# Causal attention: the mask is added by VectorE on the way to SBUF instead of by a matrix product on TensorE

## The reference, cut to what matters

```
q = (x @ w_q).reshape(bs, n, h, hd); k = ...; v = ...      # 16 heads of 64
dot = jnp.einsum('bqhd,bkhd->bhqk', q * scale, k * scale)
causal = jnp.tril(jnp.ones((n, n), dtype=bool))
dot = jnp.where(causal, dot, -inf)
att = jax.nn.softmax(dot, axis=-1)
out = jnp.einsum('bhqk,bkhd->bqhd', att, v).reshape(bs, n, h * hd)
return out @ w_u + b_u
```

## Time and profile before

| | |
|---|---|
| median of 3 runs | 1931.3 us (1929.0 to 1939.09) |
| the profiled execution | 1936.66 us, span 1934.9 us |
| granted TensorE clock, mean | 0.969 |
| causal stage in the span | from the first transfer at 4.57 us to the last addition at 367.2 us |
| PE busy | 1807.5 us of the span (93%) |
| DVE, ACT, POOL busy | 1334.9, 658.5, 266.6 us |

### The profile page before, as it was taken

The page is one execution under the profiler, slowest core; times in us unless marked ns, Lnnn a source line. Parts: engine busy times, 40 slices in busy tenths (PEclk is TensorE's granted clock), DMA queues, the critical chain, the costliest instruction groups (busy, mean ns, idle before and its releaser), DMA issues. The chain is left out here.

```text
span 1934.9 us, 44403 instructions
## 1 busy us (share of the span) xinstructions
PE 1807.5 (93%) x17091; PEld 1540.5 (80%) x17091; DVE 1334.9 (69%) x3641; ACT 658.5 (34%) x1523; POOL 266.6 (14%) x200
## 2 busy tenths in 40 slices
PE   5999999789877999999999889988999999999998
PEld 4888788567666888988888777767888888888887
DVE  4656664467658888988988848855766666666664
ACT  2444443244353112202321236645333323233332
POOL 3222333301010000000000058811000000000000
PEclk9999999799878999999999989998999999999999
DMA  4000000222033000000000130001121111112101
GB/s 164 2 1 0 0 0 1 49 58 56 20 81 62 7 0 5 5 5 0 5 5 0 37 87 2 1 26 24 26 32 16 30 19 22 27 16 33 16 1 44
DMA packets 139265, 47.73 MB, mean 25 GB/s; under 512 B 108178, under 2 KB 138418, under 8 KB 139186
## 3 DMA queue, kind: packets, MB, share of 16 engines
q1 hardware_dynamic: 139186, 46.66, 10.6%
HBM read 42.43 MB, written 4.19 MB: 24 GB/s over the span
## 5 line engine op out<-in xcount | busy, mean ns | idle before, releaser
L2988 ACT ACTIVATE m_silu<-m_gate 128x512 f32<-128x512 f32 x136 | 81.4, 599 | 379.7 <-PE m_gate L630 379.7
L3069 DVE TENSOR_TENSOR m_act_up<-m_silu,m_up 128x512 f32<-128x512 f32 x136 | 93.5, 688 | 168.7 <-PE m_up L630 125.3
L3053 DVE SCALAR_TENSOR_TENSOR g_x<-m_y,m_combine,g_x 128x256 f32<-128x256 f32 x272 | 118.9, 479 | 52.1 <-PE m_y L630 50.5
L246 ACT ACTIVATE a_prob<-a_score,a_neg_max 128x128 f32<-128x128 f32 x256 | 90.4, 365 | 162.6 <-DVE a_neg_max L236 162.6
L630 PE MATMUL f_act<-f_hT_pair_high,f_kiT_high 128*128 128x256 f32 x448 | 127.5, 285 | 0.3
L2564 PE MATMUL f_out<-f_ko,f_gel 128*128 128x256 f32 x512 | 123.7, 390 | 2.1 <-issue 1.4
L630 PE MATMUL f_act<-f_hT_pair_low,f_kiT_high 128*128 128x256 f32 x448 | 124.4, 278 | 0.0
L630 PE MATMUL f_act<-f_hT_pair_high,f_kiT_low 128*128 128x256 f32 x448 | 123.8, 276 | 0.0
L2625 ACT ACTIVATE f_gel<-f_act 128x512 f32<-128x512 f32 x128 | 76.6, 598 | 122.9 <-PE f_act L630 102.4
L2564 PE MATMUL f_turn<-f_ko,f_gel 128*128 128x256 f32 x512 | 112.1, 379 | 0.0
L2564 PEld LDWEIGHTS f_turn<-f_ko,f_gel 128*128 128x128 f32 x512 | 97.2, 190 | 13.2
(11 more groups left out here) (439 smaller groups left out, 5201.6 us busy)
## 6 DMA issues: line engine op xcount, KB each, us to landing
f_gel<-in_L_ffn_key_in SPq DMA_DIRECT2D x16, 256.0 KB, 4.5
f_ko<-in_L_ffn_key_out SPq DMA_DIRECT2D x2, 2048.0 KB, 19.3
g_shared<-in_ctx SPq DMA_DIRECT2D x8, 256.0 KB, 2.7
fp_wq_nat<-in_L_ffn_w_q SPq DMA_DIRECT2D x8, 256.0 KB, 3.1
h_kept<-fp_hT SPq DMA_DIRECT2D x8, 256.0 KB, 2.6
g_shared<-h_kept SPq DMA_DIRECT2D x8, 256.0 KB, 3.0
g_ctx_next<-in_ctx SPq DMA_DIRECT2D x8, 256.0 KB, 2.6
g_ctx_all<-in_ctx SPq DMA_DIRECT2D x1, 2048.0 KB, 9.9
```

The costliest lines, as they stand in the source:

```text
L246: last = act.activation(self.prob[:, u % 4, j, :], self.score_bank[u % 2][:, j // 2, (j % 2) * P:(j % 2 + 1) * P], ACT.Exp, bias=self.neg_ ...
L2988: act.activation(silu[:, m, :], gate_bank[m][:, :], ACT.Silu).then_inc(silu_ready[m].sem, 1)
L3053: last = dve.scalar_tensor_tensor(x[:, tile, :], y_bank[n][:, t * D:(t + 1) * D], weight, x[:, tile, :], ALU.mult, ALU.add)
L3069: dve.tensor_tensor(act_up[:, m, :], silu[:, m, :], up_bank[m][:, :], ALU.mult) \
```

## The change

The two mask products per unit go. The score products write their banks directly. VectorE adds the mask, now one float32 block of 128x128 used for all four blocks of the unit, to the scores in PSUM and writes the sum into the unit's probability buffer in SBUF; it waits for its own addition, then takes the maximum from there. ScalarE reads its exponential's input from that buffer and writes the result over it. TensorE's wait before the scores of a unit is now for the addition of two units before (the banks have been read then), not for the exponentials. The wait for a free probability buffer moves from ScalarE's queue to VectorE's. `stage_constants` fills and cuts one matrix less, and the mask is 128x128. No transfer is added, removed or moved.

```diff
 pe_scores:
-            pe.wait_ge(self.exp_ready.sem, self.exp_ready.at(i, u - 1))
-        ident_bf, mask_bf = self.mask
-        for a in range(2):
-            pe.matmul(self.score_bank[n][:, a, 0:2 * P], ident_bf[:, :], mask_bf[:, :], start=True, stop=False,
-                      skip_group_check=True)
+            pe.wait_ge(self.masked.sem, self.masked.at(i, u - 1))
...
-                                 kT[par][rows, 2 * g + t, b * P:(b + 1) * P], start=False, stop=True,
+                                 kT[par][rows, 2 * g + t, b * P:(b + 1) * P], start=True, stop=True,
...
-    def dve_max(self, dve, i, u):
+    def dve_max(self, dve, i, u, first=False):
+
         dve.wait_ge(self.scored.sem, self.scored.at(i, u + 1))
-        dve.tensor_reduce(self.neg_max[:, u, :].rearrange("p (a t) -> p a t", a=2), self.head_scores(u % 2),
-                          AX.X, ALU.max, negate=True).then_inc(self.max_ready.sem, 1)
...
+        if not first:
+            dve.wait_ge(self.transposed.sem, self.transposed.at(i, u - 3 if u != 2 else 0))
+        prob = self.prob[:, u % 4, :, :]
+        dve.tensor_tensor(prob.rearrange("p (a t) k -> p a t k", a=2), self.head_scores(u % 2),
+                          self.mask[:, :].unsqueeze(1).unsqueeze(1).broadcast_to([P, 2, 2, P]), ALU.add) \
+            .then_inc(self.masked.sem, 1)
+        dve.wait_ge(self.masked.sem, self.masked.at(i, u + 1))
+        dve.tensor_reduce(self.neg_max[:, u, :], prob, AX.X, ALU.max, negate=True).then_inc(self.max_ready.sem, 1)
...
 act_exp:
-        if not first:
-            act.wait_ge(self.transposed.sem, self.transposed.at(i, u - 3 if u != 2 else 0))
         for j in range(4):
-            last = act.activation(self.prob[:, u % 4, j, :], self.score_bank[u % 2][:, j // 2, (j % 2) * P:(j % 2 + 1) * P],
-                                  ACT.Exp, bias=self.neg_max[:, u, j:j + 1], accum_out=self.row_sum[:, u, j:j + 1])
+            last = act.activation(self.prob[:, u % 4, j, :], self.prob[:, u % 4, j, :], ACT.Exp, bias=self.neg_max[:, u, j:j + 1], accum_out=self.row_sum[:, u, j:j + 1])
...
 stage_constants:
-            for m in (ident, ident_bf, causal_bf):
+            for m in (ident, causal_mask):
                 pool.memset(m[:, :], 0.0).then_inc(filled, 1)
...
-            for m in (ident, ident_bf):
-                pool.affine_select(out=m[:, :], in_=m[:, :], compare_op=ALU.not_equal, fill=1.0, base=0,
-                                   pattern=[[-1, P]], channel_multiplier=1)
...
-            pool.affine_select(out=causal_bf[:, :], in_=causal_bf[:, :], compare_op=ALU.is_ge, fill=NEG, base=0,
-                               pattern=[[0, 2], [-1, P]], channel_multiplier=1)
...
+            pool.affine_select(out=causal_mask[:, :], in_=causal_mask[:, :], compare_op=ALU.is_ge, fill=NEG, base=0,
+                               pattern=[[-1, P]], channel_multiplier=1)
```

More of the change, by code:

```diff
@@ L197, in __init__ @@
         self.scored = s.counting("scored", UNITS)
+        self.masked = s.counting("masked", UNITS)
         self.max_ready = s.counting("max_ready", UNITS)
@@ L343, in act_first @@
     def act_first(self, act):
-        self.act_exp(act, 0, 0, first=True)
-        self.act_exp(act, 0, 1, first=True)
+        self.act_exp(act, 0, 0)
+        self.act_exp(act, 0, 1)
     def on_act(self, act, i, before, after):
@@ L358, in dve_first @@
     def dve_first(self, dve):
-        self.dve_max(dve, 0, 0)
-        self.dve_max(dve, 0, 1)
+        self.dve_max(dve, 0, 0, first=True)
+        self.dve_max(dve, 0, 1, first=True)
         self.dve_normalise(dve, 0, 0)
@@ L383, in on_dve, with stage_causal_attention @@
             self.links.end()
-def stage_causal_attention(nc, x, ident, ident_bf, mask_bf, x_in, w_q, w_k, w_v, w_u, b_u, load_next):
+def stage_causal_attention(nc, x, ident, mask, x_in, w_q, w_k, w_v, w_u, b_u, load_next):
     HD = 64
@@ L412, in chunk_of @@
             return part[:, c // 2, 4 * (c % 2):4 * (c % 2) + 4, :].rearrange("p t q -> p (t q)")
-        att = CausalAttention(s, ident, (ident_bf, mask_bf), lambda c: chunk_of(attnT, c),
+        att = CausalAttention(s, ident, mask, lambda c: chunk_of(attnT, c),
                               vector_copies=(0, 2, 4, 6))
@@ L3085, in _, with stage_constants @@
             all_experts(dve, expert_on_dve)
-def stage_constants(nc, ident, ident_bf, causal_bf, head_mask, ones_row):
+def stage_constants(nc, ident, causal_mask, head_mask, ones_row):
     with ExitStack() as ctx:
@@ L3101, in _ @@
                 pool.memset(m[:, :], 1.0).then_inc(filled, 1)
-            pool.wait_ge(filled, 5)
-            for m in (ident, ident_bf):
-                pool.affine_select(out=m[:, :], in_=m[:, :], compare_op=ALU.not_equal, fill=1.0, base=0,
-                                   pattern=[[-1, P]], channel_multiplier=1)
-            pool.affine_select(out=causal_bf[:, :], in_=causal_bf[:, :], compare_op=ALU.is_ge, fill=NEG, base=0,
-                               pattern=[[0, 2], [-1, P]], channel_multiplier=1)
+            pool.wait_ge(filled, 4)
+            pool.affine_select(out=ident[:, :], in_=ident[:, :], compare_op=ALU.not_equal, fill=1.0, base=0,
+                               pattern=[[-1, P]], channel_multiplier=1)
+            pool.affine_select(out=causal_mask[:, :], in_=causal_mask[:, :], compare_op=ALU.is_ge, fill=NEG, base=0,
+                               pattern=[[-1, P]], channel_multiplier=1)
             pool.affine_select(out=head_mask[:, :], in_=head_mask[:, :], compare_op=ALU.is_ge, fill=0.0, base=0,
@@ L3124, in decoder @@
         stored = s.sem("stored")
-        ident_bf = s.sb("ident_bf", [P, P], BF16)
-        causal_bf = s.sb("causal_bf", [P, 2 * P], BF16)
+        causal_mask = s.sb("causal_mask", [P, P])
         shared = Shared(s, "shared", 3072)
```

6 lines of the change are left out of this document (3 added, 3 removed).

## The result

Median of 11 runs each: 1944.84 us after (1941.52 to 1951.07), 1934.44 before (1929.00 to 1939.09), ratio 1.0053 with a 95% interval of 1.0040 to 1.0066: 10.4 us longer. That is inside the wide range forecast (1926 to 1947), outside the range of the forecast case itself (1930 to 1943), and on the edge of the 0.5% (the interval lies on both sides of it). The profiled execution took 1943.92 us, span 1942.2, which is 7.3 more than before's 1934.9; the forecast was 4.0 more. In the experiments, the ratios leave out one run of e6 (9558.9 us) and one of before (2912.6 us) that stand far off.

A forecast was written before the change was run, and what follows sets the result against it. TensorE bounds steps 0 to 3, while DVE's chain ends level with it in steps 4 to 7. Sum: -6.2 + 7.0 + 3.1 + 0.7 - 0.6 = +4.0 us on 1931.3, 1935.3; range 1930 to 1943, wide 1926 to 1947.

The forecast's parts named there:

- forecast case: The prediction's own case for the whole kernel: 1935.3 us, range 1930 to 1943, chance 0.75.
- the pairs: Seven pairs before the last: 6.2 us won in steps 0 to 3, 7.0 lost in steps 4 to 7.
- the last pair: Final pair without ring work: six DVE additions lengthen the chain, 3.1 us later (2.3 to 4.4, slow clock perhaps 1 more).
- the start: Before the first pair: 0.7 us lost to DVE's additions and maxima, 0.6 won by GpSimd's smaller fills and selects.
- GpSimd blocks addition and maximum: Rival: GpSimd's splits also hold DVE's addition and maximum, delaying ScalarE's copy; +10 to +11 us, 1942; chance 0.08.
- the two handovers: Ring to scores in steps 0 to 3, 0.23 us won each; DVE's copy to transposes in steps 5 and 7, 0.50 late.
- T+0.09 to T+3.84: Steps 4 and 5, T being the ring's end: scores start at T+0.09, the next transposes at T+3.84, 0.50 us late.
- the 0.6 us that GpSimd wins at the start: Kernel start: one fill and one select fewer, and smaller ones, 0.6 us before the first transfer is issued.
- perhaps 1: Last pair: what a slow clock there might add, in us, on top of the 4.4 upper case.
- PE is the bound after all: Rival: all 64 units save 0.23 to 0.32 us and the addition hides everywhere; -15 to -20 us, chance 0.10.
- The clock falls in pairs 0 to 6: Rival: longer transpose waits in steps 5 and 7 bring half clock to some pairs; 1943 to 1960 us, chance 0.07.
- DVE's queue backs up: Layer normalisation behind longer step 5 delays a ring copy: 0.3 us more per pair, +6 in all, inside the range.

The follow-up runs named there:

- e6: The changed kernel with one more wait, so GpSimd's second output-weight split follows DVE's last input-weight subtraction; 1941.1 us, ratio 1.0036 to before.
- e5: The kernel before with one more wait, so GpSimd's second output-weight split follows DVE's last input-weight subtraction; 1928.7 us, ratio 0.9976.
- e12: The changed kernel with 20 unread filler products on PE between the scores of units 1 and 2 of the first pair; 1942.5 us, ratio 1.0035 to before.
- e1: The kernel before with its mask products removed and nothing in their place (softmax over unmasked scores); 1929.0 us, ratio 0.9974.
- e2: The changed kernel with the mask products of before put back, so the mask is added twice; 1952.8 us, ratio 1.0089 to before.
- e11: The kernel before, all masks by products, with DVE's and ScalarE's late steps reordered and GpSimd's second split made to wait; 1928.5 us, ratio 0.9973.
- e3: The changed kernel with DVE adding masks only for units 2 to 5, mask products elsewhere and in the last pair; 1935.9 us, ratio 1.0014 to before.
- e4: The changed kernel with mask products for units 0 and 1 of the first pair and 2 to 7 of the last; 1938.9 us, ratio 1.0029 to before.
- e7: The changed kernel, DVE normalising and copying before addition and maximum (steps 4, 6), ScalarE copying before exponentials (5, 7); 1940.8 us, ratio 1.0036 to before.
- e9: As e7, with DVE's copy of finished head outputs also ahead of addition and maximum in steps 4 and 6; 1935.4 us, ratio 1.0004 to before.

## Why the prediction came out as it did

**The size.** Forecast were 4.0 us more, measured 7.3 in the profiled executions and 10.4 in the medians. Of the terms of the sum, the pairs (0.8 forecast, 1.09 measured) came close, the last pair (3.1, measured 3.85) was sized too low, and the start (+0.1, measured 2.18) was wrong. The base of 1931.3, from three runs, lay 3.1 under the median of eleven. The other 3.1 us, between 7.3 and 10.4, are in no term. That 10.4 equals the +10 to +11 of the rival in which GpSimd blocks addition and maximum is coincidence: its mechanism didn't occur (below).

**Right:** the direction, the place, and the two handovers. A score group begins 0.21 behind the last ring product (about 0.1 of it gap, as taken from the earlier trace rows), which saves 0.24 against 0.23 predicted. In step 4 the transposes come 3.73 behind the scores' start (194.05 to 197.78), where the prediction had T+0.09 to T+3.84, 3.75. The transposes wait 1.20 and 1.29, the normalisation takes 1.60, the period is 41.95. The values product of step 7 starts at 209.87 without a wait, 0.77 behind the start of ScalarE's copy:

```profile
207.54 0.40 ACT L246 ACTIVATE a_prob<-a_prob,a_neg_max 128x128 f32<-128x128 f32 x1 [1.68 <-DVE a_neg_max L241]
...
209.10 0.57 ACT L268 COPY a_probT<-a_probT_bank 128x512 f32<-128x512 f32 x1
```

The pairs' own sum was 0.8 us predicted (7.0 less 6.2) and 1.09 measured; 0.09 of DVE's backlog (below) comes once a pair.

**The start, +0.1 predicted, +2.18 measured.** Two steps failed. The 0.7 for addition and maximum was right (first normalisation 47.11 before, 47.77 after). But the change also moves a wait: the third score group waits for the addition now, not for the exponentials. Before's PE and after's:

```profile
46.92 0.39 PE L224 MATMUL a_score<-g_causal_bf,g_ident_bf 128*128 128x256 bf16 x2 [1.44 <-ACT a_prob L246]
47.24 0.72 PE L229 MATMUL a_score<-a_kT,a_qT 64*128 64x128 f32 x8
47.95 0.65 PE L262 MATMUL a_probT_bank<-g_ident,a_prob 128*128 128x128 f32 x4
```

```profile
45.18 0.71 PE L226 MATMUL a_score<-a_kT,a_qT 64*128 64x128 f32 x8 [0.48 <-DVE a_prob L237]
```

The group comes 2.06 us earlier, and nothing is left to break PE's wait for the normalisation: 1.44 us and a group became 2.71 in one piece. The first transposes come 0.65 later (48.60 against 47.95). The other 1.53 of the 2.18 are the half clock behind them. I had weighed the clock for the pairs and the last pair only. Whether the joined wait brought it down stays open: e6 has the same wait and no fall, e5 the shorter one and a fall. Without a fall in either kernel the start costs 0.65.

The other failed step is the 0.6 us that GpSimd wins at the start and that did not stay. The first transfer goes out 0.61 earlier (3.96 against 4.57). GpSimd's first step of the layer normalisation comes 0.42 earlier (9.53 against 9.95), DVE's first copy of queries 0.21 (21.85 against 22.06), its copy behind the lock 0.22 (34.90 against 35.12), its last ring copy before the scores 0.05 (42.42 against 42.47). So it melts on both sides of the lock, and no run shows what takes it.

**The last pair, +3.1 predicted, +3.85 measured.** PE's waits there:

```profile
350.28 0.63 PE L261 MATMUL a_probT_bank<-g_ident,a_prob 128*128 128x128 f32 x4 [1.61 <-ACT a_probT L268]
...
355.89 1.09 PE L261 MATMUL a_probT_bank<-g_ident,a_prob 128*128 128x128 f32 x4 [1.94 <-ACT a_probT L268]
...
362.95 1.09 PE L261 MATMUL a_probT_bank<-g_ident,a_prob 128*128 128x128 f32 x4 [2.52 <-ACT a_probT L268]
```

and DVE:

```profile
353.72 1.53 DVE L254 TENSOR_TENSOR a_prob<-a_prob,a_norm 128x512 f32<-128x512 f32 x1
...
359.24 0.69 DVE L237 TENSOR_TENSOR a_prob<-a_score,g_causal_mask 128x512 f32<-128x512 f32 x1 [0.47 <-PE a_score L226]
```

Measured from the residual mark, these transposes, which wait for ScalarE's copies, come 1.34, 1.87 and 3.84 later than before's (7.09, 12.70, 19.76 against 5.75, 10.83, 15.92). The normalisation at 353.72 is held for 0.84, as the prediction had it (up to 0.8). Two terms were missing. The group at 355.89 runs at 1.2 GHz (1.09 for 0.63), now ahead of unit 7's scores, and DVE waits 0.47 us for those at 359.24: that is the clock's part on the path, of which the prediction had said "perhaps 1" without putting it in the sum. And the exponentials were costed at nothing, by a cast of 512 columns. They take 391 ns, 365 before, and follow each other by 0.39 instead of 0.345: 0.18 us a unit. Here the Trainium skill ("VectorE: DVE Perf Modes", the TRN2 errata) had it right, with 52 cycles more for ScalarE from SBUF, an estimate of 43 ns at the 1.2 GHz of its table. The trace agrees from start to start (45 ns); the duration shows less (26). My row was too far: a cast of 512 columns doesn't show what an exponential of 128 with a sum does. With both terms in, 3.1 would have become 3.1 + 0.5 + 3 x 0.18 = 4.1, an estimate. Elsewhere the exponentials stay hidden; the values product above shows it.

The 3.85 is one execution's. With the same code in the last pair, e6 took 33.40 us and e12 32.32, where after took 31.13: 6.1 and 5.0 more than before's 27.28. In e6 the last of these transposes stands at the same 19.76 behind the mark, and the other 2.3 us lie in the output projection, which ran at half clock (granted 0.50 in 361.56 to 363.56). In e12 the clock fell earlier, behind the wait of 1.78 us for DVE's copy at 345.44 that after and e6 passed at full clock.

**The rivals.** *PE is the bound after all*: dead, by e1 (10.6 us of the stage, not 15 to 20) and by after's 19.1 us of waits. *GpSimd blocks addition and maximum*: dead. All 64 additions take 679 to 694 ns and all 64 maxima 686 to 689, also where they begin inside a split; only the normalisation, with two SBUF inputs, is held (1.60), and in the start the two 2048-column subtractions (6.40 for 2.28). That is the rule of the Trainium skill ("SBUF — State Buffer", "Who interferes with whom"), and the trace agrees. For one SBUF input the page excepts DVE's two-port modes, which the prediction left out; no run here tells whether the 1384 ns of the earlier trace rows was such a case. *The clock falls in pairs 0 to 6*: not in the steady ones, granted 1.00 with waits of 1.20 and 1.29. Pair 0 opens with half clock in after, which I had named as a sign of being wrong (and in five of the fourteen executions in all), and the last pair has more of it. *DVE's queue backs up*: by 0.09 us (step 7 waits 1.29, step 5 1.20), not 0.3.

**Not foreseen: instructions are fetched again.** Between 560 and 1100 us, in the product-key stage that nobody touched, the queue of instruction fetches of before, after and e1:

```profile
q8 instruction: 11, 0.18, 0.1%
```

```profile
q8 instruction: 65, 1.06, 0.8%
```

```profile
q8 instruction: 66, 1.08, 0.8%
```

11 packets, 65 and 66. The products into `f_out` (line 2563, 2564 before) take 489.5 us from the first to the end of the last before and 490.9 after. Every kernel whose pair loop has no (or fewer) mask products shows 105 or 106 packets over the whole span, and 490.7 to 493.5 us; before, e2, e5 and e11, which have them all, show 52 and 489.5 to 489.8. e1 against before is this one edit (490.7 against 489.5). So taking the products out goes with 0.9 to 4.0 us more in that stage, in every execution; that the packets are the cause, and why fewer instructions make more of them, was not tested.

**Open.** 7.1 of the 7.3 us between the profiled executions lie in the stage; the 1.4 of the product-key stage is made up elsewhere in this pair of executions (the rest differs by 0.2). The 3.1 from there to the 10.4 of the medians are shown by no trace. Before's profiled execution was 2.2 us above its median and had the lock, after's was 0.9 below its own. The stretch behind the stage took 1561.6 to 1572.7 us in the twelve experiments, without order by kernel, so one span says it only to some microseconds. Against before, the stage marks of e1, e3 and e4 are also 5 to 9 us better than their medians. Some 5.5 of e4's are the race at its start; for the others I have no cause that a run shows. The falls of the clock at both ends, 1.5 and up to 2.3 us with the same code, are of this size.

## What to carry to other kernels

Work taken from the busiest engine is won only at the handovers where that engine ends last: look for them step by step, and price the receiving engine's steps the same way, since here four steps of eight gave 0.24 us each and the other four cost 0.5 twice, with DVE at 69% of the span. When a wait is removed by reordering, name the next instruction of the same queue before counting the gain (e7 got 0.3 of 2.2 us, e9 found the next one on ScalarE). Price the ends of a stage by themselves, with the clock as a chance and not as a certainty: the same wait there went with a fall, worth 1.5 us, in three executions of four. Where two engines share a lock, look in several executions who wins it before comparing spans.

## What was not expected of the hardware

- DVE's and GpSimd's large subtractions, both with two SBUF inputs, block each other: DVE's took 6.40 us for 2.28 when GpSimd began 0.3 us earlier, and GpSimd's 6.53 for 4.6 the other way round. Without this race before's start is 5.6 us shorter and its whole time 4.6 (1.9 to 7.4, by the ratio).
- The granted clock behind the same code differs from execution to execution: behind a wait of 2.71 us TensorE fell to 1.2 GHz for about 3.4 us in after and stayed at 2.4 GHz in e6; behind a wait of 1.44 it stayed in before and fell in e5. The waits of 1.20 and 1.29 in the steady pairs left it at 1.00 in pairs 1 to 6 of after.
- An exponential of 128 columns with a sum costs 26 ns more from SBUF (391 against 365) and 45 ns more from start to start; a cast of 512 columns shows 1 ns.
- Taking the mask products out of the pair loop goes with 54 more instruction packets in a later loop, and with 1.4 us there.
